# Where a layer norm's statistics are taken, and in which order keys and queries are projected, in an eight-layer gated cross-attention and mixture-of-experts kernel

## The reference, cut to what matters

```python
def _layernorm(x, axis=-1, eps=1e-05):
    m = jnp.mean(x, axis=axis, keepdims=True)
    v = jnp.var(x, axis=axis, keepdims=True)
    return (x - m) / jnp.sqrt(v + eps)
...
x = x + jnp.tanh(g_xattn[0]) * _L0_xattn_ref(_layernorm(x), ctx_1024, mask, mask, ...)
x = x + jnp.tanh(g_ffn[0]) * _L0_ffn_ref(_layernorm(x), ...)      # LoRA adapters, 8 experts
x = x + jnp.tanh(g_xattn[1]) * _L1_xattn_ref(_layernorm(x), ctx_1024, ctx_1024, ...)
x = x + jnp.tanh(g_ffn[1]) * _L1_ffn_ref(_layernorm(x), ...)      # 64 experts, 8 chosen, and one shared
x = x + jnp.tanh(g_xattn[2]) * _L2_xattn_ref(_layernorm(x), ctx_1024, ctx_1024, mask, ...)
x = x + jnp.tanh(g_ffn[2]) * _L2_ffn_ref(_layernorm(x), ...)      # 14 experts, one chosen
x = x + jnp.tanh(g_xattn[3]) * _L3_xattn_ref(_layernorm(x), ctx_1024, ctx_1024, ...)
x = x + jnp.tanh(g_ffn[3]) * _L3_ffn_ref(_layernorm(x), ...)      # an attention of x with itself, then 8 experts
```

## Time and profile before

| what | value |
|---|---|
| time before, median of 3 runs | 1445.65 us (1440.37, 1445.65, 1448.24) |
| the profiled execution, its own time | 1440.67 us |
| its span in the profile | 1438.8 us |
| PE busy | 1137.6 us (79%), 10478 matmuls |
| DVE busy | 909.3 us (63%) |
| ACT busy | 782.5 us (54%) |
| POOL busy | 552.9 us (38%) |
| TensorE's mean granted clock | 0.889 of full speed |
| DMA | 95.72 MB, 67 GB/s over the span |

### The profile page before, as it was taken

The page is one execution under the profiler, slowest core; times in us unless marked ns, Lnnn a source line. Parts: engine busy times, 40 slices in busy tenths (PEclk is TensorE's granted clock), DMA queues, the critical chain, the costliest instruction groups (busy, mean ns, idle before and its releaser), DMA issues. The chain is left out here.

```text
span 1438.8 us, 31204 instructions
## 1 busy us (share of the span) xinstructions
PE 1137.6 (79%) x10478; PEld 535.6 (37%) x10478; DVE 909.3 (63%) x1691; ACT 782.5 (54%) x1459; POOL 552.9 (38%) x604
## 2 busy tenths in 40 slices
PE   2668667886299999997677679999778848786997
PEld 1334444454134444444123423333344522233332
DVE  3758648884666666667698434444668658963443
ACT  1257412773155555553288347777537624872775
POOL 1205102551055555554045047777302102212675
PEclk9779977997599999998599769999969986995999
DMA  8731004100044444442510000000151022100001
GB/s 258 244 122 33 2 1 149 48 18 1 20 138 127 132 124 132 125 130 72 202 47 17 1 0 0 0 0 1 58 165 47 3 93 71 46 3 0 0 1 29
DMA packets 95699, 95.72 MB, mean 67 GB/s; under 512 B 16618, under 2 KB 76194, under 8 KB 94306
## 3 DMA queue, kind: packets, MB, share of 16 engines
q1 hardware_dynamic: 93298, 80.90, 18.7%
q10 hardware_dynamic: 2288, 13.31, 2.5%
HBM read 75.23 MB, written 18.61 MB: 65 GB/s over the span
## 5 line engine op out<-in xcount | busy, mean ns | idle before, releaser
L732 ACT ACTIVATE work<-ps 128x384 f32<-128x384 f32 (+1 forms) x640 | 303.9, 533 | 184.3 <-PE ps L588 115.0
L829 DVE TENSOR_REDUCE bmax<-ps 128x6 f32<-128x768 f32 (+1 forms) x320 | 334.6, 1056 | 80.9 <-PE ps L566 55.0
L1276 PE MATMUL ps<-ao,wf 128*128 128x512 f16 x1320 | 344.1, 387 | 11.2 <-DVEq L1367 6.6
L1296 PE MATMUL ps<-work,wf 128*128 128x512 f16 x924 | 253.4, 383 | 4.4 <-POOL work L1265 4.4
L1265 POOL TENSOR_TENSOR work<-work 128x512 f16<-128x512 f32 x176 | 203.9, 1159 | 108.1 <-ACT work L1346 108.1
L1389 DVE TENSOR_TENSOR work<-work,ps 128x512 f32<-128x512 f32 x176 | 120.9, 688 | 166.7 <-POOL work L1265 133.8
L1265 POOL TENSOR_TENSOR work<-Ks,work 128x512 f16<-128x512 f32 x132 | 153.1, 1160 | 146.7 <-ACT work L1346 146.7
L1276 PEld LDWEIGHTS ps<-ao,wf 128*128 (+1 forms) x1320 | 115.8, 99 | 195.0 <-issue 84.6
L867 POOL TENSOR_SCALAR mx<-bmax 128x16 f16<-128x16 f32 x80 | 25.0, 313 | 379.5 <-DVE bmax L835 214.6
L577 PE MATMUL ps<-Qs,Ks 32*128 32x256 f16 x640 | 121.5, 289 | 58.6 <-DMA Qs<-mxT 24.4
L1338 ACT ACTIVATE work<-ps,cols 128x512 f32<-128x512 f32 x176 | 120.8, 688 | 67.7 <-PE ps L1288 47.8
(11 more groups left out here) (166 smaller groups left out, 1605.6 us busy)
## 6 DMA issues: line engine op xcount, KB each, us to landing
Qs<-scrC SPq DMA_DIRECT2D x256, 128.0 KB, 3.0
Qs<-scrQ SPq DMA_DIRECT2D x40, 256.0 KB, 3.1
Ks<-scrK SPq DMA_DIRECT2D x40, 256.0 KB, 3.4
scrK<-work SPq DMA_DIRECT2D x60, 128.0 KB, 2.1
scrQ<-work SPq DMA_DIRECT2D x60, 128.0 KB, 2.2
Qs<-mxT SPq DMA_DIRECT2D x320, 1.0 KB
wf<-in_L_w ACTq DMA_DIRECT2D x2, 1792.0 KB, 11.0
wf<-in_L_wg ACTq DMA_DIRECT2D x1, 2112.0 KB, 10.2
```

The lines of the kernel that those rows point to most:

```text
L732: act.activation(prob[:, g % 8, 0:W1], ps[:, 4 + g % 3, 0:W1], ACT.Exp, scale=float(att["dk"]) ** -0.5).then_inc(exped, 1)
L829: dve.tensor_reduce(bmax[:, n // 4 % 2, 2 * (n % 4):2 * (n % 4) + 2, 0:NB], ps[:, b0:b0 + 2, 0:W1].rearrange("p i (n w) -> p i n w", n=NB) ...
L1276: ins = pe.matmul(out, weight_parts(which, wpart, j), xh[:, xpart, c * CH:(c + 1) * CH], start=(i == 0), stop=(i == 2))
L1296: ins = pe.matmul(ps[:, YB + c % 2, :], weight_parts(m_["mats"] - 1, wpart, s), hparts[:, (m + r) % 4, hpart, :], start=(opens and i == 0) ...
```

## The change

**Statistics where `x` gets its last addition.** `norm_statistics`, `norm_vector`, `norm_pool` and the norm stage are gone. After each chunk's addition to `x` (in attentions 0 to 3, the adapter stage and the expert stages 1 and 2) DVE drains and takes the chunk's four `bn_stats` (`added_chunk`). After the third chunk it computes the variance of 12 tiles, after the fourth that of the last 4; POOL takes the power in the same two groups at the stage's end (`inverse_deviation`). The next stage begins with `apply_norm`, chunk by chunk. The first statistics are taken in the setup.

**Keys and queries in turns.** The order of projection, splitting and writing is now k0 k1 q0 k2 q1 k3 q2 q3 (`PARTS`), with keys in banks 0 to 3 and queries in banks 4 to 7, and the norm, transposes and copies of a chunk between them. A load waits only for the writes that it needs. The values are projected in the first four steps of the row loop, in the place of `keep_warm`, and their bias is added by DVE in steps 1 to 4. Attention 4 applies its own norm.

**Setup.** The mask comes as one row and as 16 rows; a matmul with a row of ones spreads the row over 128 partitions (four matmuls, ACT copies), a transpose makes the columns. SP no longer waits for the constant rows in the setup but ahead of the first load of attention 0. `sel` is loaded in step 56 of attention 0, without layer 1's part (736 KB in place of 1760 KB). The temporary of the output moves from `xn` or `ctxT` to `ao`.

```diff
@@ setup_stage, sync
-            with nc.allow_non_contiguous_dma(reason="one mask value a descriptor, 2048 of them once"):
-                sp.dma_start(qmaski, dr["mask"].rearrange("b (t p) -> p (b t)", p=P)).then_inc(s_in, 16)
+            sp.dma_start(maskrow, dr["mask"].rearrange("b (o s) -> o (b s)", o=1)).then_inc(s_keys, 16)
+            sp.dma_start(mask16, dr["mask"].rearrange("b (t p) -> (b t) p", p=P)).then_inc(s_keys, 16)
...
-            sp.dma_start(maski, dr["mask"].rearrange("b s -> (b s)").partition_broadcast(P)).then_inc(s_in, 16)
...
-            sp.wait_ge(s_const, 128)
@@ setup_stage, tensor
+            pe.wait_ge(s_kept, 2)
+            for c in range(NC):
+                pe.matmul(ps[:, 4 + c, :], ones, keeprow[:, c * CH:(c + 1) * CH], start=True, stop=True).then_inc(s_spread, 1)
+            pe.wait_ge(s_copied, 1)
+            pe.transpose(ps[:, 0, 0:NT], keep16, ident[0:16, 0:16]).then_inc(s_q, 1)
@@ setup_stage, vector, at its end
+            dve.wait_ge(s_x, 16)
+            for c in range(NC):
+                chunk_statistics(nc, st, dve, c)
+            variance(nc, st, dve, slice(0, NT), s_var)
@@ new
+def chunk_statistics(nc, st, dve, c):
+    for t in range(4 * c, 4 * c + 4):
+        dve.bn_stats(st["stats"][:, t, :], st["x"][:, t * D:(t + 1) * D])
+
+FIRST_TILES, LAST_TILES = slice(0, 12), slice(12, 16)
+
+def added_chunk(nc, st, dve, c, s_var):
+    dve.drain()
+    chunk_statistics(nc, st, dve, c)
+    if c == NC - 2:
+        variance(nc, st, dve, FIRST_TILES, s_var)
+    if c == NC - 1:
+        variance(nc, st, dve, LAST_TILES, s_var)
+
+def inverse_deviation(st, pool, s_var):
+    for n, at in enumerate((FIRST_TILES, LAST_TILES)):
+        pool.wait_ge(s_var, n + 1)
+        pool.tensor_tensor(st["rstd"][:, at], st["mom"][:, 5, at], st["neghalf"][:, at], ALU.pow)
...
+PARTS = [("k", 0), ("k", 1), ("q", 0), ("k", 2), ("q", 1), ("k", 3), ("q", 2), ("q", 3)]
@@ attention_stage, tensor
-            for i in range(NC):
-                project(i)
-            for c in range(NC):
-                project_values(c)
-            turn_normed(0)
-            turn_normed(1)
-            project(NC)
...
+            for p in range(len(PARTS)):
+                if not own and p in (1, 2, 4, 6):
+                    c = p // 2
+                    turn_normed(st, pe, c, 4 + c, s_xn, s_xt)
...
+                project(p)
...
-                if n < LEAD:
+                if n < NC:
+                    project_values(n)
+                elif NC < n < LEAD:
                     keep_warm(n)
@@ attention_stage, vector, ahead of the row loop
-            if not own:
-                norm_statistics(nc, st, dve, s_var)
...
-            for c in range(NC):
-                take_low(NC + c)
-                add_value_bias(c)
+            for p in range(len(PARTS)):
+                if not own and p in (1, 3, 5):
+                    apply_norm(st, dve, (p + 1) // 2, s_xn)
...
+                if by_pool(p):
+                    keep_keys(p)
+                else:
+                    take_low(p)
@@ attention_stage, vector, in add_output and in the row loop
                 dve.scalar_tensor_tensor(xc, fresh, st["gate"][:, a:a + 1], xc, ALU.mult, ALU.add)
-                dve.drain()
+                added_chunk(nc, st, dve, c, s_var)
...
+                if 1 <= n <= NC:
+                    add_value_bias(n - 1)
@@ attention_stage, sync
-            if a == 0:
-                sp.dma_start(st["sel"][:], dr["sel"]).then_inc(st["wsem"][0], 16)
...
-            for i in range(NC + 2):
-                write(i)
+            for p in range(3):
+                write(p)
             sp.wait_ge(bias_written, 16)
+            if a == 0:
+                sp.wait_ge(st["s_const"], 128)
             load(0)
-            write(NC + 2)
+            write(3)
             load(1)
-            write(NC + 3)
+            write(4)
+            write(5)
             load(2)
+            write(6)
             load(3)
+            write(7)
...
+                if a == 0 and n == 56:
+                    for first, last in ((0, SEL_OFF[1]), (SEL_OFF[2], SEL_N)):
+                        sp.dma_start(st["sel"][:, first:last], dr["sel"][:, first:last]).then_inc(st["wsem"][0], 16)
```

325 lines of the change are left out of this document (153 added, 172 removed).

## The result

The changed kernel takes 1422.14 us, the median of 4 runs (1420.25 to 1424.77), against 1446.03 for the kernel before (1440.37 to 1448.24, 4 runs). The ratio is 0.984, with a 95% interval of 0.981 to 0.988. So it is 24 us faster. Forecast were 1401 us and a gain of 45. The sign was right and the time is inside the range of 1386 to 1427, but only about half of the gain came.

A forecast was written before the change was run, and what follows sets the result against it. No engine was full; stretches where every engine waits for one chain were taken as the bound. Terms of 7.0 + 12.9 - 2.7 + 17.6 + 7.4 + 3.3 + 7.6 - 10 gave 43 us, hence 1401 us, range 1386 to 1427.

The forecast's parts named there:

- Handover to a route: From last addition to norm, 3.4 us in place of 7.7, gaining 12.9 us over three routes.
- the rival of a fixed cost: POOL's power costs the same on 4 columns, 13 us more over seven handovers: 1414 us, chance 0.15.
- Setup: Setup stage ends at 23.6 in place of 30.6, gaining 7.0 us (4 to 9).
- Attention 0: Ninth exponential 39.3 us after the stage's start in place of 56.9, gaining 17.6 us; lower bound 10.
- the second rival: First maxima in attentions 0, 2 and 3 still wait for all the weights: 1414 us, chance 0.15.
- The wide reading: In attention 0, maxima would be seen only once weights ahead of them are written, speaking against the 17.6 us gain.
- The queues of an attention: With the new order, the first row matmul comes 15.6 us after an attention's start in place of 21.8.
- The values: Value biases in the row loop add 2.6 us to 12.3: 14.9 from first row matmul to first exponential.
- my clock rival: PE at half clock until values are projected: 1440 us, chance 0.04; in some stages only, 1421, chance 0.08.
- Attention 1 with the adapter: Stage starts 6.4 us later by the adapter's longer tail and wins 3.7 back: -2.7 us.
- Statistics where they stand: Statistics behind additions in attentions 0 to 3 and expert stages 1 and 2 cost 10 us (bounds 0 and 22).
- Attention 4: From last addition to ninth exponential, 37.6 us in place of 45.2, gaining 7.6 us.

The follow-up runs named there:

- old order: Changed kernel with keys and queries projected, split and written as before (all keys, then all queries), first load behind 18 writes: 1438.43 us.
- halves: Changed kernel with each weight matrix issued in two halves, spread ahead of exponential pairs 1 to 16 in attentions 0, 2 and 3: 1406.62 us.
- all together: Changed kernel with weights in halves, values in the prelude's gaps, last loads and writes from ACT, adapter additions interleaved, first statistics before mask tables: 1383.07 us.
- the two tails: Changed kernel with adapter additions in turns with the multiplications, and setup statistics and POOL's power ahead of their tables: 1412.27 us.
- another bank: Changed kernel with the matmuls without use in steps 5 to 10 writing to bank 4 in place of bank 7: 1417.92 us.

## Why the prediction was right in sign and half wrong in size

**Handover to a route: right.** 3.8, 3.4 and 3.4 us in the three routes, where 3.4 was forecast. The power on 4 and 12 columns was read rightly as mostly work per column, and the rival of a fixed cost (1414) did not happen. The third route shows only 1.4 of its 4.3 us in the table, because the half clock lasted 34.1 us through it, where before full clock lay between two stretches of 17.1 and 23.9. The other kernels bear this out. The stretch took 22.5 to 22.7 us in the three traces in which full clock came back in it (old order, halves, all together), and 25.6 in the eight with the statistics in place in which it did not.

**Setup: the term was mis-sized, 2.4 for 7.0.** The step that failed is that `x` lands at 13.6 and that "from there DVE does what it did after 25.70". `x` landed at 16.3, 2.7 us later. And DVE does its tables first, whose last load landed at 17.84; in my sum I had let the tables' loads, ACT's, be done. With the statistics ahead of the tables, in the kernel of the two tails, the setup ended at 25.6. Over the eight traces with this setup the gain is 0.4 to 2.4. The durations behind it were right (DVE 7.0 us and POOL 3.0).

**Attention 0: the second rival happened.** I gave 39.3 us for the ninth exponential and named 46.8 as the lower bound if the maxima wait for all the weights. In time they did, and it came at 49.1. The step that failed is "a 1 KB maximum passes within a few large packets of half a microsecond". From 66 to 74 us q10 moved 215 packets and q1 53:

```profile
q10 hardware_dynamic: 215, 3.36, 98.4%
q1 hardware_dynamic: 53, 0.00, 0.4%
```

Yet the turns were equal. The packets of the trace show each of these DMAs as 16 packets of 64 bytes and four of 4 bytes, its signals: it runs on four of the 16 DMA engines (its source is four partitions). Of q10's 215 packets an engine had 13, and q1's 53 on four engines are also 13 each. As long as weights stood in q10, a packet of 64 bytes had to let one of 16.9 KB, 0.63 us, pass each time. The fourth maximum DMA (issued at 57.66) moved its data from 61.92 to 64.71, four packets 0.63 to 0.64 us apart on each engine, and its last signal came at 65.68; PE went on at 65.81. The four of the second unit were complete at 68.21, 71.03, 73.91 and 76.44, some 3 us each, and PE went on at 76.53. The first three DMAs of the first unit, ahead of the weights, had taken 1.7 us or less. So what my step missed is that a maximum is not one packet but four and a signal on each of its engines, and that a unit is four such DMAs behind each other: 20 turns.

The wide reading of the Trainium skill ("DMA: Bandwidth & Descriptors", Queues, rings and completion order), by which the maxima's signals would be held back until the weights ahead of them are written, does not fit this trace. The first DMA of the second unit was issued at 58.24, behind the second weight matrix (58.08), and was complete at 68.21, before that matrix at 70.97. All but the last DMA had their signals 0.3 to 0.6 us behind the packet that carries them; the last had them 0.5 to 1.7 us behind it. The price of the second rival was about right, but its cause was the turns. That PE went on near 65.9 and 76.5 is therefore no proof of a wait for the weights. In the kernel before, equal turns are enough as well: a load of keys on all 16 engines, issued at 60.73 ahead of all the weights, landed only 21.3 us later, with the last of them:

```profile
Ks<-scrK SPq DMA_DIRECT2D x1, 256.0 KB, 21.3
```

The kernel with the weights in halves shows what matters for the kernel: with less of them in flight the wait is gone. It was there in attention 2 too, where I had put 15.6 us from the first row matmul to the first exponential, and a little in attention 3 (14.9): they took 23.0 and 19.4, and 17.9 and 17.3 with the halves. Whether maxima in fewer or wider DMAs would do the same was not tried.

**The queues of an attention: right.** First row matmuls came 16.3, 15.3, 16.1 and 15.3 us after the starts of attentions 0 to 3, against 16.5, 15.6, 17.5 and 15.6 in the forecast.

**The values: the term was too small, by a second effect.** I had 2.6 us. From the first row matmul to the first exponential it is 16.2 in place of 12.3, so 3.9: DVE's biases took what was forecast, and then the first maxima, turned at 239.1, waited for SP, whose last writes were out at 241.0. I had noted that SP's last write would come at 26 to 27.5 us and used it only for the weights. Another 2.1 to 2.5 us in each of attentions 0, 1, 3 and 4 (1.2 in attention 2) went to the clock in this pair of traces, since the half clock lies over more of the exponentials. This is akin to my clock rival, at a smaller price. I looked for it in the prelude and in thin row steps; it was in what the earlier start uncovers. With the adapter (2) and the third route (3), the clock makes some 15 of the 27 us that this pair lacks to the forecast's 43, an estimate from the stages above. There is one trace of the kernel before, so how often its exponentials escape the half clock is not known; in the changed kernels' traces attention 1 took 15.0 or 15.4 us from pair 4 to 16 three times and 17.2 to 18.1 nine times. Attention 3 is the plain case: 7.5 us sooner at the first row matmul, 0.4 us later at the last addition. There the weights take part too: 24.7 us from the first row matmul to pair 4, 21.6 in attention 1.

**Attention 1 with the adapter: -8.9 for -2.7** (-4.1 with its share of the statistics). The tail is 8.4 in place of 6.4. In the adapter the half clock lasted 8.4 us (4.1 before), and PE's work there came out 2 us later. Two other kernels with this adapter, in which it lasted 3.8, have a tail of 6.3, so the 6.4 of the sum was right for an equal clock:

```profile
190.00:198.00 8.00, 8.00 (x21) 4.12 (x21) 3.37 (x3) 1.17 (x2) 0.00 (x0) 0.50 0.01 2
198.00:206.00 8.00, 8.00 (x55) 6.03 (x54) 3.28 (x8) 1.17 (x2) 0.00 (x0) 1.00 0.00 0
```

The rest is the previous point.

**Statistics where they stand: the term was too large, 0 to 3 for 10.** The additions of chunks 0, 1 and 2 in the attentions are as far apart as before (5.9 us in attention 0). Only the last addition, which has the variance of 12 tiles ahead of it, follows the third by 8.7, 8.0, 7.6 and 8.1 us in attentions 0 to 3, in place of 7.3, 7.3, 8.5 and 7.3. With the statistics taken out again attention 0 gained 0.8 us, within the scatter, and the expert stages gained only their tails. DVE's gaps covered nearly all of them, close to my bound of 0. This error went the other way: it hid a part of what the other terms lacked.

**Attention 4: right in the total**, 7.8 for 7.6, by parts that cancel. The first row matmul came 21.7 us after the last addition (forecast 21.9), the first exponential 17.4 behind it (forecast 15.7), so only 6.1 were gained up to there. Another 1.8 came later, where I had put nothing; their cause stays open.

So the time fell into the range with several terms off in both directions; that the total came within 21 us of 1401 is no sign that the terms were right. Two bounds of mine were also added up slightly wrong (46.8 should be 46.3, and -22 about -21); neither moves the forecast.

## What to carry to other kernels

When a wait is shortened, look at what is late next on every engine and queue, and then at the clock. A first row matmul that came 6.5 us sooner in attention 1 brought the first exponential only 2.7 us sooner, because DVE now had the value biases there and the first small transfers stood behind the last writes of their own queue; and in this pair of traces the half clock took the rest. Small latency-bound transfers should not share the DMA engines with megabytes that nobody needs yet: cut the large load into halves and spread them. Count a small transfer in packets for each DMA engine, for each of them lets a large one pass. Work that is taken off a wait should go into a gap of its own engine: from the first row matmul to the first exponential attention 1 took 16.2 us with the value biases in the row steps that DVE paces, and 14.7 with them in the gaps between keys and queries. And look at the mean clock of all runs before a stage of one trace is explained.

## What the runs showed of the hardware

POOL's power to -1/2 took 1.01 us on 128 x 4, 2.27 to 2.30 on 128 x 12 and 2.90 to 3.30 on 128 x 16. Two queues with large and small packets took equal turns on a DMA engine: 111 to 107 packets where both used all 16 engines, 215 to 53 where the small ones, of 64 bytes, used four. A DMA of 1 KB on four engines took some 3 us beside packets of 16.9 KB, and 1.7 without. TensorE's clock fell to half 9 to 12 us after the first row matmul in all five attentions with values in the first steps (the changed kernel and the one with another bank) and 2.6 to 5.8 us after it without them, whether PE ran three matmuls without use in each step, two or none. The half clock then lasted between 10 and 38 us, in one place of the program or another and in kernels that hardly differ there. What sets this length the runs leave open. In attentions 1 and 3 it was worth 2.2 to 3 us when it lay over the exponentials from pair 4 on, in the third route 3 us, and in the adapter 0.5 us for each of its microseconds. These are the sizes by which stages without an edit differ between two traces.
